# Flamingo block on one core: attention products regrouped by type, output bias in bfloat16, router and positions later

## What is computed

```python
q, k = apply_rope(layernorm(x)), apply_rope(ctx)          # v is ctx without rope
scores = einsum('bhqd,bhkd->bhqk', Q, K) / sqrt(8)        # per head 128 x 128
out = einsum('bhqk,bhkd->bhqd', softmax(scores), V)
x = x + tanh(g_xattn) * (out.reshape(B, S, D) @ Wo_w.T + Wo_b)
xn = rms_norm(layernorm(x), norm_scale)
ids = top_k(xn @ w_router.T, 2); c = softmax(...)[ids]    # 8 experts
y_e = w_down[e] @ (val * silu(gate)),  (val, gate) = w_up[e] @ xn
x = x + tanh(g_ffn) * (sum over the two experts c * y + layernorm(x))
```

## Time and profile before

| what | value |
|---|---|
| median of 3 runs | 574.02 us (564.71 to 576.14) |
| the profiled execution | 566.83 us, its span 565.0 us |
| mean granted clock of TensorE | 0.813 |
| busy: TensorE, VectorE, ScalarE, GpSimd | 82%, 55%, 45%, 36% |
| attention batches | up to 338.9 us |
| expert tiles | 367 to 540 us |

### The profile page before, as it was taken

The page is one execution under the profiler, slowest core; times in us unless marked ns, Lnnn a source line. Parts: engine busy times, 40 slices in busy tenths (PEclk is TensorE's granted clock), DMA queues, the critical chain, the costliest instruction groups (busy, mean ns, idle before and its releaser), DMA issues.

```text
span 565.0 us, 13155 instructions
## 1 busy us (share of the span) xinstructions
PE 463.1 (82%) x3820; PEld 302.2 (53%) x3821; DVE 308.2 (55%) x1119; ACT 257.0 (45%) x578; POOL 204.7 (36%) x196
## 2 busy tenths in 40 slices
PE   6579999989799799897979672099999999999910
PEld 2335554645455455445445342067877777778710
DVE  5275786966466467546547134145555555555525
ACT  2316575754354355444334422045555555555400
POOL 4251232334334335325411506524444444444410
PEclk9779999988578679588567555589999999999955
DMA  5524141443644203104100101221211111121049
GB/s 154 130 53 106 40 121 32 125 115 88 173 109 127 72 11 104 40 12 114 50 21 2 40 1 39 87 67 58 60 55 55 54 57 53 55 57 45 23 156 291
DMA packets 53314, 43.15 MB, mean 76 GB/s; under 512 B 7776, under 2 KB 50019, under 8 KB 53267
## 3 DMA queue, kind: packets, MB, share of 16 engines
q1 hardware_dynamic: 46834, 32.40, 21.2%
q0 software_dynamic: 4416, 8.63, 4.7%
q10 hardware_dynamic: 2016, 1.52, 1.1%
HBM read 18.45 MB, written 11.75 MB: 53 GB/s over the span
## 4 chain that ended last, share of the span: by engine, by line
PE 72%; DVE 6%; issue 5%; DMA 5%; another core or an unknown queue 4%; ACT 3%; POOL 2%; SPq 1%; ACTq 1%; POOLq 0%; DVEq 0%
PE bank L1347 9%; PE bank L1325 8%; PE bank L1327 8%; PE bank L1149 7%; PE bank L1136 6%; PE bank L1123 5%; PE bank L1337 4%; PE bank L1166 4%; DMA yl<-result_dram 2%; PE bank L1182 2%; PE bank L1183 2%; PE bank L1093 2%; PE bank L1103 2%; PE bank L1111 2%
## 5 line engine op out<-in xcount | busy, mean ns | idle before, releaser
L734 DVE TENSOR_REDUCE nmx<-bank 128x4 f32<-128x512 f32 x128 | 86.6, 684 | 79.3 <-PE bank L1123 64.9
L468 POOL DMA_INDIRECT result_dram<-ys,yi x72 | 70.4, 978 | 108.1 <-ACT ys L665 103.9
L524 ACT ACTIVATE pt<-bank 128x512 f32<-128x512 f32 x128 | 72.7, 596 | 32.5 <-PE bank L1136 32.4
L411 POOL DMA_INDIRECT slots_dram<-xr,slu x64 | 62.5, 976 | 32.5 <-issue 17.2
L1347 PEld LDWEIGHTS bank<-wf_sb,hT 128*128 128x128 f32 (+1 forms) x432 | 57.3, 192 | 21.3 <-issue 17.2
L1021 DVE TENSOR_TENSOR hh<-sg,bank 128x352 f32<-128x352 f32 x72 | 37.5, 521 | 55.9 <-PE bank L1327 45.1
L1347 PE MATMUL bank<-wf_sb,hT 128*128 (+1 forms) x432 | 61.5, 279 | 2.0 <-DVE hT L1031 1.8
L1149 PE MATMUL bank<-pt,v 128*9 128x128 f32 x1024 | 60.8, 316 | 0.3
L1123 PE MATMUL bank<-ks,qs 62*128 62x128 bf16 x512 | 57.5, 243 | 3.9 <-DVE nmx L734 2.1
L1325 PE MATMUL bank<-wf_sb,xT 128*128 x144 | 55.7, 469 | 0.0
L1327 PE MATMUL bank<-wf_sb,xT 128*128 x144 | 55.0, 464 | 0.0
(11 more groups left out here) (154 smaller groups left out, 757.4 us busy)
## 6 DMA issues: line engine op xcount, KB each, us to landing
qs<-parts SPq DMA_DIRECT2D x48, 128.0 KB
ks<-parts SPq DMA_DIRECT2D x42, 128.0 KB
xs<-slots_dram SPq DMA_DIRECT2D x72, 66.0 KB
yl<-result_dram SPq DMA_DIRECT2D x8, 512.0 KB, 6.0
wf_sb<-in_wup SPq DMA_DIRECT2D x8, 352.0 KB
x_sb<-in_x SPq DMA_DIRECT2D x8, 256.0 KB, 4.1
ctx_sb<-in_ctx_in SPq DMA_DIRECT2D x8, 256.0 KB, 3.8
out<-x_sb SPq DMA_DIRECT2D x8, 256.0 KB, 4.6
```

What stands on the lines that cost most here:

```text
L411: nc.gpsimd.indirect_dma_start(out=slots_dram, out_offset=bass.IndirectOffsetOnAxis(ap=slu[:, c % 2, k, kk:kk + 1], axis=0), in_=xr[:, c % ...
L468: nc.gpsimd.indirect_dma_start(out=result_dram, out_offset=bass.IndirectOffsetOnAxis(ap=yi[:, r:r + 1], axis=0), in_=ys[:, r, :], in_offse ...
L524: nc.scalar.activation(pt[:, 4 * g:4 * g + 4, :], STB[g % 2][:, :].rearrange("p (h s) -> p h s", h=4), ACT.Exp, scale=SCORE_SCALE).then_in ...
L734: nc.vector.tensor_reduce(nmx[:, b % 2, at:at + 4], SB[g % 2][:, :].rearrange("p (h s) -> p h s", h=4), AX.X, ALU.max, negate=True).then_i ...
```

## The change

It moves calls in the loops of TensorE, ScalarE, VectorE and GpSimd, and makes the output bias another product. The diff, cut to the parts on which the prediction speaks (the loops of ScalarE and VectorE move with TensorE's):

```diff
+            def bias_parts():
+                ch = Chain(dve, d_bo, 0)
+                ch.link(nc.vector.tensor_tensor(bop[:, 0, :], SMALL[0:3, 0:D], bo_sb[:, :], ALU.add))
+                ch.link(nc.vector.tensor_copy(bhigh[:, 0, :], bop[:, 0, :]))
+                ch.link(nc.vector.tensor_tensor(bop[:, 1, :], bop[:, 0, :], bhigh[:, 0, :], ALU.subtract))
+                ch.link(nc.vector.tensor_copy(bhigh[:, 1, :], bop[:, 1, :]))
...
             def project_out(b):
                 pe.wait_ge(a_aT, b + 1)
-                mm(SMALL[:, D:2 * D], ones[0:1, :], bop[:, :], start=True, stop=False)
-                mm(SMALL[:, D:2 * D], onT[:, :], wo_sb[:, :], start=False, stop=True).then_inc(pe_o, 1)
+                mm(SMALL[:, D:2 * D], onT[:, :], wo_sb[:, :], start=True, stop=False)
+                mm(SMALL[:, D:2 * D], onesb[0:3, :], bop3[:, :], start=False, stop=True).then_inc(pe_o, 1)
...
-            for b in range(B + CH + 1):
+            for b in range(B + 2 * CH):
                 c, u = b // CH, b % CH
                 if real(b):
                     scores_by_key(b, 0)
                     scores_by_key(b, 1)
                 if real(b + 2):
                     scores(b + 2, 0)
+                    scores(b + 2, 1)
                 if real(b + 1):
                     transpose_maximum(b + 1)
                 if real(b - 1):
                     heads_by_query(b - 1)
-                if real(b + 2):
-                    scores(b + 2, 1)
-                if real(b):
-                    weighted_values(b, 0)
-                    scores_by_key(b, 2)
...
                 if real(b):
-                    weighted_values(b, 1)
+                    weighted_values(b, 0)
+                    scores_by_key(b, 2)
                     scores_by_key(b, 3)
                 if real(b + 2):
                     scores(b + 2, 2)
+                    scores(b + 2, 3)
+                if real(b):
+                    weighted_values(b, 1)
                 if real(b - 1):
                     transpose_attended(b - 1)
-                if real(b + 2):
-                    scores(b + 2, 3)
+                if u == 1 and there(c + 2):
+                    transposes_ctx(c + 2, PR)
+                if u == 3 and there(c - 1):
+                    transpose_rows(c - 1)
+                if u == 0 and there(c - 2):
+                    router(c - 2, b)
+                if u == 2 and there(c - 2):
+                    positions(c - 2, b)
                 if real(b):
                     weighted_values(b, 2)
+                    weighted_values(b, 3)
                 if real(b - 1):
                     project_out(b - 1)
-                if u == 0 and there(c - 2):
-                    positions(c - 2, b)
...
-                        scatter(c - 3, (2, 3))
-                if u == 1 and there(c - 1):
-                    power2(c - 1)
+                        scatter(c - 3, (0, 1, 2))
+                if u == 1:
+                    if there(c - 1):
+                        power2(c - 1)
+                    if there(c - 3):
+                        scatter(c - 3, (3,))
...
-            scatter(NCH - 3, (2, 3))
+            scatter(NCH - 3, (0, 1, 2))
             power2(NCH - 1)
+            scatter(NCH - 3, (3,))
```

More of the change, by code:

```diff
@@ L602, in _ @@
                     middle(c + 1, 1)
-                if u == 2 and there(c - 1):
-                    rows(c - 1, (0, 1))
-                if u == 3 and there(c - 1):
-                    rows_transposed(c - 1)
-                if real(b):
-                    exponent(b, 2)
-                if u == 0 and there(c + 1):
                     values(c + 1, PR)
@@ L614, in _ @@
                     high(c + 2, 0, PR)
+                if u == 3 and there(c + 2):
+                    high(c + 2, 1, PR)
+                if u == 3 and there(c - 1) and c < NCH:
+                    rows(c - 1, (2, 3))
+                if real(b):
+                    exponent(b, 2)
+                if u == 2 and there(c - 1):
+                    rows(c - 1, (0, 1))
                 if real(b - 1):
                     attended(b - 1)
-                if u == 2 and there(c - 1) and c < NCH:
-                    rows(c - 1, (2, 3))
-                if u == 0 and there(c - 2):
+                if u == 1 and there(c - 2):
                     expert_exp(c - 2)
@@ L926, in _ @@
                     maximum(b + 2, 1)
-                if u == 0 and there(c - 2):
+                if u == 1 and there(c - 2):
                     choose_values(c - 2)
+                if u == 2 and there(c - 2):
+                    choose_masks(c - 2)
                 if real(b - 1):
@@ L932, in _ @@
                     shift(c + 2)
-                if u == 1 and there(c - 2):
+                if u == 2 and there(c - 2):
+                    choose_sum(c - 2)
+                if u == 3 and there(c - 2):
                     place_rows(c - 2)
@@ L955, in _ @@
                     maximum(b + 2, 3)
-                if u == 0 and there(c - 2):
-                    choose_sum(c - 2)
-                if u == 1 and there(c - 2):
+                if u == 2 and there(c - 2):
                     probabilities(c - 2, 1)
@@ L961, in _ @@
                     widen(c + 3)
[L962 to L963 removed]
+                if u == 3 and there(c - 2):
+                    place_numbers(c - 2)
+                    probabilities(c - 2, 2)
                 if real(b - 1):
                     add_attention(b - 1)
+                if u == 2 and there(c - 2):
+                    take_positions(c - 2)
                 if u == 0 and there(c - 2):
[L967 to L971 removed]
+                    take_scores(c - 2)
                 if real(b - 1):
@@ L979, in _ @@
                     rotate_q(c + 2)
-                if u == 3 and there(c + 2):
-                    remainder(c + 2, 1, PR)
             ch = Chain(dve, d_tc, 0)
@@ L1158, in heads_by_query @@
                 c, u = b // CH, b % CH
-                if u == 3 and there(c - 1):
-                    pe.wait_ge(d_sc, c)
                 if u == 0 and there(c - 2):
+                    pe.wait_ge(d_sc, c - 1)
+                if u == 2 and there(c - 2):
                     pe.wait_ge(d_tp, c - 1)
```

85 lines of the change are left out of this document (38 added, 47 removed).

## The result

The changed kernel takes **544.3 us** (median of four runs, 543.6 to 547.7) against 571.9 for the kernel before (four runs, 564.7 to 576.1): a ratio of 0.961, with an interval of 0.951 to 0.971. Some runs of a kernel are disturbed (a lower clock, over 1.5% above that kernel's fastest run), and every ratio here leaves them out: of the kernel before it counts 564.7 and 569.8 us here, and runs of 520.6 to 527.8 us in the last group of experiments. The forecast was 532 with a range of 507 to 560. The direction and the range held; the gain was 27.6 us where the sum had 37.6 to 42. The profiled execution took 543.7 us (span 541.9); against the one of before (span 565.0) that is 23.1 us.

A forecast was written before the change was run, and what follows sets the result against it. The prediction took TensorE's products and the clock to set the time. Its terms summed to 37.6 us off the profiled 566.8, giving 529; allowing for the 574.0 median of three runs, it forecast 532, range 507 to 560.

The forecast's parts named there:

- the two products' steps: TensorE, each batch: paired scores save 0.73 us at the high clock, 1.28 low; the bfloat16 output bias 0.25 and 0.45.
- that case: Rival: score pairs on TensorE do not overlap where they now stand, 29 us of gain missing, 559 us; chance 0.05.
- Rows' wait: New wait at u = 3 for the expert rows, moved one batch later: 0.8 us a stretch, bounds 0 and 2.
- Positions and router later: Router and positions move by one and two batches; nobody waits for them in the steady stretches.
- the rival of the waits: VectorE and ScalarE become the bound; half of the 37.6 us comes back, 550 us; chance 0.18.
- Such stalls are in the run before, and stay: GpSimd scatter bursts, now six and two a stretch: zero cost in the steady part, bounds -2 and +3 us a stretch.
- I take 0.8 instead of 1.08: High-clock batches: of 1.08 us saved on TensorE, 0.8 reaches the end, as VectorE becomes a near bound.
- The first stretch: Attention batches from 47 to 72 us: forecast gain 3.0 us, 4 x 0.8 less a little.
- 257.5 to 297.2: Attention stretch at mean clock 0.66: forecast gain 5.5 us, from 1.3 high-clock and 2.7 low-clock batches, less 0.5.
- The end: Last scatters to expert tiles: two more scatters behind the last power, chunk 6's slots later; 3 us lost, bounds 2 and 8.
- the forecast's 3 us: Stretch 136 to 257.5 us: 3.0 us gained from a higher mean clock as idle time goes, bounds 0 and 8.
- It did not stay up: Rival: denser work keeps 2.4 GHz through the batches that now run low, 17 us more, 515 us; chance 0.13.

The follow-up runs named there:

- the two product edits alone: Kernel before with score groups in pairs and the output bias as three bfloat16 parts, no moves: 546.5 us, ratio 0.958.
- The experiment: Changed kernel with a 1.67 us GpSimd operation between the three pairs of the six scatters at u = 0: 526.1 us, ratio 0.918.
- The gaps: 526 us kernel with chunk 5's scatters all ahead of the last power and two GpSimd operations among chunk 7's scatters: 522.0 us, ratio 0.914.
- the kernel of 546.5 us: Kernel before with score groups in pairs and the output bias as three bfloat16 parts, nothing moved: 546.5 us, ratio 0.958.

## Why the prediction was right, and where its sum was not

**Right, and shown.** That TensorE's products set the time: the two product edits alone give the ratio of the whole change (0.958 and 0.961). The sizes of the two products' steps, at either clock. That the pairs overlap where they stand: sixteen products in 0.56 us. The Trainium skill ("TensorE: Matmul & The Clock Gate", Part 3, what overlaps and what doesn't) has matmuls start and end in program order, by which I had put a block at 1.05 us and the kernel at 559; the trace does not bear that out (a block took 0.56), and taking the pairs apart cost 17 us. My two prices of that case did not agree either: 559 takes the term as nothing, while 1.05 us a block made it a loss of 0.3 us a batch. Rows' wait: 1.0 us in three stretches where I had 2.4. Positions and router later: nothing, as forecast.

**In part luck.** From 72 us to the last power TensorE's idle time grew by 19 us (34.6 to 53.6 in the table). That is what the rival of the waits had priced, half of 37.6, with a chance of 0.18. Against it, TensorE's busy time fell by 50.6 us in these stretches, where the forecast had taken 37.6 us off their lengths, clock and waits included. From 136 to 257.5 us it fell by 24.9; the terms of the products give 17.6 (6 x 1.08 and 6 x 1.86), and the granted clock rose there from 0.75 to 0.84. How much of the surplus is the clock isn't shown. Two errors of opposite sign kept the total in the range.

**The step that failed: "Such stalls are in the run before, and stay ... I cost this at zero".** They stayed but grew. In chunks 3 to 5 the stand was 8.9 us and became 13.1, 1.4 us a stretch and inside my bounds of -2 and +3; but I had set the term to zero with no row for it. I had also read the earlier trace rows wrongly: 7.09 us is how long VectorE was idle. The products of that group (L1123) ran from 279.34 to 279.94, so it started some 6 us late, and TensorE waited 5.1 us there, its longest wait in the attention batches of before. The experiment prices it: 18 us of 544 go with the stands. Of these the stands of chunks 3 to 6 themselves are 13.4 us (17.6 in sum before the edit, 4.2 after it); the rest I can't split between other waits and the clock, which rose at once.

**"At the high clock ... I take 0.8 instead of 1.08".** I saw that VectorE was near and took too little off. TensorE's work in the four batches from 72 us fell by 4.75 us, more than my 4.3, and the stretch by 2.0, 0.5 us a batch. The waits are for a landing (1.2), ScalarE's exponents (1.7) and VectorE's query (0.8). My own question, what is late next, I had asked of the rows only. The steady stretches show the same two engines with 6.2 and 5.0 us. I had also set 33 us of TensorE's work against VectorE's 24 for four batches at the low clock. The stretches are a mixture of both clocks, and measured 27.5 us (82.38 / 3) beside 24.4: VectorE was nearly as close a bound there. Four steady batches took 36.4 us and not 34.

**The first stretch** lost 1.0 us where I had it gain 3.0: one of its batches ran at a granted clock of 0.80, against 1.00 in the trace of before, and just ahead of it TensorE had waited 1.4 us for the stack of keys to land, in front of the regrouped scores. That the one brought the other wasn't tested.

**257.5 to 297.2** gained 9.1 and not 5.5, probably because of a row of eight scatters, beside which TensorE waited 5.1 us there and which moved on to the next stretch with the router.

**The end** lost 7.6 us, at the edge of my bounds (2 to 8). I had two causes at 3 us together. Missing was that the two scatters behind the power also hold VectorE's last rows until they land (2.90 us), and that the pad stores meet a row of sixteen instead of eight (7 us more). The gaps won back 3.9 us of it.

**The clock** rose from 0.813 to 0.849 in the mean, as the forecast's 3 us supposed; in 136 to 257.5 from 0.75 to 0.84. It did not stay up. One argument of mine on it was wrong: that only the stretches with the wait of the earlier trace rows or a burst run below 1.00. The stretch from 72 us has that wait too (1.1 us before L1193, shown above) at a granted clock of 1.00.

**Open.** What in an unbroken row of scatters holds the other engines up isn't shown; the runs show only that gaps take it away. The first two chips give 570 us for the kernel before, and the third 526. That rows of scatters cost TensorE nothing on the third is shown by its traces; that this is the whole difference is not. Whether the moves help or cost there is not measured either: the changed kernel itself was not run on that chip.

## What to carry to other kernels

Price an edit of the busiest engine twice: what it takes off that engine, and what remains of this once the engines it hands to are next in line; at the high clock here, 1.19 us a batch became 0.5. A row of DMAs issued by GpSimd is an event for all engines: look in the trace at who waits "<- remote" or "<- issue" beside one, and try gaps before you divide or move the row. And take the kernel before along on every chip: a stand of 18 us on one chip wasn't there to be won on another.

## What the runs showed of the hardware

- While GpSimd issues indirect scatters without a gap (one each 1.26 us), engines that wait for TensorE's results start late: VectorE 4.9 us after its product's end beside a row of six in the changed kernel (136.37 to 141.31) and 6.4 with the pairs apart, ScalarE 7.3 us beside a row of eight (263.33 to 270.58 in the kernel of 546.5 us). They start around the last scatter or up to 2 us after it. TensorE's own loss is about the same for rows of four and of six (2 to 5.2 and 3.6 to 6.2 us); with a GpSimd operation of 1.67 us between the pairs 0.9 to 1.3 is left, and has a named cause.
- SyncE's four stores of 66 KB, with the loads of registers between them, take 4.8 us with gaps among the scatters, 6.0 to 6.6 beside a row of eight, and 12.7 to 14.7 within a row of sixteen, where SyncE's instructions start 0.70 us apart.
- This was so on two chips and not on a third, where a row of eight held nobody up and the pad stores took 3.8 to 4.2 us beside a row of sixteen. The scatters' own pace was the same on all.
